# Flamingo block on one core: first sequence's queries moved tile to tile, keys split first, one query stack moved, transfers reordered

## The reference

```python
qs = relu(layernorm(x)).reshape(bs, ts, 16, 32)
ks = vs = relu(ctx).reshape(bs, ts, 16, 32)
att = softmax(einsum('bthf,byhf->bhty', qs, ks) / sqrt(32))
out = einsum('bhty,byhf->bhtf', att, vs).reshape(bs, ts, -1)
x = x + tanh(g_xattn) * relu(out @ ffn_w.T + ffn_b)
# feed-forward part, on n = layernorm(x) and n one token earlier
xr, xk = mu_r * n + (1 - mu_r) * n_prev, mu_k * n + (1 - mu_k) * n_prev
x = x + tanh(g_ffn) * sigmoid(xr @ W_r.T) * (square(relu(xk @ W_k.T)) @ W_v.T)
```

## Time and profile before

| what | us |
|---|---|
| median of 3 runs | 2684.31 |
| profiled execution, its own time | 2686.47 |
| its span | 2684.7 |
| TensorE matmul busy | 2597.9 (97%) |
| VectorE busy | 2282.9 (85%) |
| ScalarE busy | 1695.4 (63%) |
| GpSimd busy | 1162.9 (43%) |

### The profile page before, as it was taken

One profiled execution on the slowest core, in us unless ns is written; L12 is line 12 of the kernel. 1 busy time (PEld: TensorE's weight loads), 2 busy tenths in 40 slices (PEclk: granted clock), 3 DMA queues, 4 the chain that ended last, 5 costly groups with the idle time before them and its releaser, 6 DMA issues. The chain is left out here.

```text
span 2684.7 us, 66755 instructions
## 1 busy us (share of the span) xinstructions
PE 2597.9 (97%) x20354; PEld 2074.9 (77%) x20354; DVE 2282.9 (85%) x4109; ACT 1695.4 (63%) x3531; POOL 1162.9 (43%) x902
## 2 busy tenths in 40 slices
PE   3799999999999999999999999999999999999998
PEld 2577778787787787787787778778778778787776
DVE  6688888888888889888888888888888888888875
ACT  4466666666666666666666666666666666666663
POOL 0144444444444444444444444444444444444434
PEclk9799999999999999999999999999999999999999
DMA  9787777777777778778778778787787787777751
GB/s 256 210 215 228 215 213 230 222 212 229 221 209 233 223 208 234 218 209 234 223 209 234 218 211 232 211 222 224 214 227 222 211 231 222 211 228 220 209 153 44
DMA packets 523216, 576.78 MB, mean 215 GB/s; under 512 B 191264, under 2 KB 422688, under 8 KB 523168
## 3 DMA queue, kind: packets, MB, share of 16 engines
q1 hardware_dynamic: 369648, 340.71, 46.5%
q10 hardware_dynamic: 153520, 235.46, 30.1%
HBM read 373.56 MB, written 201.33 MB: 214 GB/s over the span
## 5 line engine op out<-in xcount | busy, mean ns | idle before, releaser
L618 ACT ACTIVATE probs<-bank 128x512 f32<-128x512 f32 x1024 | 610.2, 596 | 523.2 <-PE bank L1103 519.7
L858 DVE TENSOR_REDUCE m_nat<-bank 128x2 fp32r<-128x512 f32 x1024 | 689.2, 681 | 76.5 <-PE bank L1091 76.3
L1091 PE MATMUL bank<-k_st,q_st 96*128 96x256 f32 x2048 | 435.1, 295 | 37.5 <-ACT bank L630 26.2
L877 DVE RECIPROCAL o_val<-bank 128x256 f32<-128x256 f32 x192 | 336.7, 1754 | 138.8 <-PE bank L1129 138.8
L1091 PEld LDWEIGHTS bank<-k_st,q_st 96*128 96x128 f32 x2048 | 362.8, 193 | 108.0 <-ACT bank L630 40.1
L1103 PE MATMUL bank<-q_st,k_st 97*128 97x256 f32 x2048 | 426.2, 290 | 8.6 <-DMA q_st<-m_t 8.2
L1103 PEld LDWEIGHTS bank<-q_st,k_st 97*128 97x128 f32 x2048 | 357.3, 191 | 85.5 <-issue 23.3
L464 POOL TENSOR_TENSOR xm<-xm 128x512 f32<-128x512 f32 x128 | 157.1, 1227 | 463.0 <-ACT xm L677 462.0
L630 ACT ACTIVATE bank<-bank,m_nat 128x256 f32<-128x256 f32 x512 | 227.6, 444 | 136.5 <-DVE m_nat L858 136.2
L431 POOL TENSOR_TENSOR o_lo<-o_mv,o_hi 128x512 fp32r<-128x512 f32 x128 | 168.6, 1317 | 304.5 <-ACT o_hi L640 302.1
L1146 PE MATMUL bank<-xk_hi,w_hi 128*128 128x256 f32 x1024 | 294.9, 288 | 1.0 <-DVE th L940 1.0
(11 more groups left out here) (94 smaller groups left out, 5945.8 us busy)
## 6 DMA issues: line engine op xcount, KB each, us to landing
q_st<-q_dram ACTq DMA_DIRECT2D x256, 256.0 KB, 4.8
k_st<-k_dram SPq DMA_DIRECT2D x256, 256.0 KB, 4.7
k_raw<-ctx_t_dram SPq DMA_DIRECT2D x256, 128.0 KB, 5.1
q_st<-q_dram ACTq DMA_DIRECT2D x256, 128.0 KB, 2.9
k_st<-k_dram SPq DMA_DIRECT2D x256, 128.0 KB, 5.0
o_dram<-o_val SPq DMA_DIRECT2D x256, 128.0 KB, 2.1
o_mv<-o_dram SPq DMA_DIRECT2D x1024, 32.0 KB, 3.1
x<-x_dram ACTq DMA_DIRECT2D x64, 512.0 KB, 6.7
```

The costliest lines, as they stand in the source:

```text
L618: nc.scalar.activation(probs[:, n // GR % 2, n % GR, :, :].rearrange("p v t -> p (v t)"), st_bank[n % 2][:, :], ACT.Exp).then_inc(exp_read ...
L858: nc.vector.tensor_reduce(m_nat[:, c % 2, n % GR, :], s_bank[n % 2][:, :].rearrange("p (u y) -> p u y", u=NU), AX_X, ALU.max, negate=True) ...
L877: nc.vector.reciprocal(o_val[:, c % 2, :], pv_bank[:, T:2 * T]).then_inc(rden_ready, 1)
L1091: mm = nc.tensor.matmul(s_bank[n % 2][:, T * u:T * u + T], q_st[0:QK, c, g, P * u:P * u + P], k_st[0:QK, c, g, :], start=True, stop=True)
```

## The change

The change has five parts.

1. The stack of query group 0 of sequence 0 is no longer written to DRAM and read back. Twelve DMAs on ScalarE's queue take rows from `q_high` (eight) and `q_raw` (four) straight to `q_st`, one for each head and each of the three places. The halving of group 0 is done by itself first (`q_hi_first`, `q_lo_first`), on both ScalarE and VectorE. `q_copy(1, ...)` waits until these DMAs have read.
2. `stack_q(i, 3)` goes, in every iteration, from behind `exponent(i, 0)` to behind `sum_exp(i, 7)`.
3. `k_halve(0)` becomes the first thing of ScalarE's iteration -2 and `k_low(0)` follows `norm_1(0)`; `k_halve(1)` and `k_low(1)` go from iteration -1 into iteration 0 (behind `sum_exp(0, 6)` and `head_max(0, 9)`).
4. SyncE's opening is reordered: the first keys are written before `load_x(1)`, and `stack_k(0, 0)` is issued before the other groups are written; `stack_k(0, 2)` and `move_m(0, 0)` come before `load_k(1)`.
5. In iteration 0, `stack_k(1, 1)` directly follows `stack_k(1, 0)`, `load_x(3)` follows `write_o(0, 0)`, and the two `read_o` of the first tile go ahead of `move_m(1, 0)`, the first of them ahead of `write_o(0, 1)`.

```diff
@@ SyncE @@
+            def write_k_first(b, par):
+                sp.wait_ge(k_hi_ready, b + 1)
+                sp.wait_ge(k_lo_ready, b + 1)
+                for half, tile in enumerate((k_high, k_raw)):
+                    sp.dma_start(k_dram[par, 0, half].rearrange("f g t -> (f g) t"),
+                                 tile[:, 0, :]).then_inc(k_first, 16)
...
+                    if first_sequence(b) and c == 1:
+                        sp.wait_ge(k_written, 32)
                     sp.dma_start(k_st[0:2 * HD, c, :, :].bitcast(F32),
...
-                    if first_sequence(b) and c == 0:
-                        sp.wait_ge(k_written, 32)
@@ opening @@
                     load_k(0)
                     load_w(range(0, 4))
+                    write_k_first(0, par)
                     load_x(1)
+                    stack_k(0, 0, par)
                     write_k(0, par)
                 elif i == -1:
-                    stack_k(0, 0, 1 - par)
                     stack_k(0, 1, 1 - par)
+                    stack_k(0, 2, 1 - par)
+                    move_m(0, 0)
                     load_k(1)
-                    move_m(0, 0)
-                    stack_k(0, 2, 1 - par)
                     load_x(2)
...
                     stack_k(1, 0, 1 - par)
+                    stack_k(1, 1, 1 - par)
                     load_k(2)
                     move_m(0, 3)
                     load_w(range(6, 7))
                     write_o(0, 0)
-                    stack_k(1, 1, 1 - par)
                     load_x(3)
+                    read_o(0, 0, 0)
                     write_o(0, 1)
                     stack_k(1, 2, 1 - par)
+                    read_o(0, 0, 1)
                     move_m(1, 0)
                     load_w(range(7, 8))
-                    read_o(0, 0, 0)
-                    read_o(0, 0, 1)
@@ ScalarE @@
+                        act.wait_ge(q_hi_first, 1)
+                        for row in (0, HD):
+                            for g in range(GR):
+                                act.dma_start(q_st[row:row + HD, 0, g, :].bitcast(F32),
+                                              q_high[g:P:GR, 0, :]).then_inc(q_stacked[0], 16)
+                        act.wait_ge(q_lo_first, 1)
+                        for g in range(GR):
+                            act.dma_start(q_st[2 * HD:QK, 0, g, :].bitcast(F32),
+                                          q_raw[g:P:GR, 0, :]).then_inc(q_stacked[0], 16)
...
             def iteration(i, par):
+                if isinstance(i, int) and i == -2:
+                    k_halve(i + 2)
                 exponent(i, 0)
-                stack_q(i, 3, par)
                 sum_exp(i, 6)
+                if isinstance(i, int) and i == 0:
+                    k_halve(i + 1)
                 exponent(i, 1)
                 split_high(i, 6, 1)
                 sum_exp(i, 7)
+                stack_q(i, 3, par)
...
-                k_halve(i + 2)
+                if not (isinstance(i, int) and i < 0):
+                    k_halve(i + 2)
@@ VectorE @@
                 head_max(i, 9)
+                if isinstance(i, int) and i == 0:
+                    k_low(i + 1)
                 stats_1(i + 2)
...
                 norm_1(i + 2)
+                if isinstance(i, int) and i == -2:
+                    k_low(i + 2)
...
-                k_low(i + 2)
+                if not (isinstance(i, int) and i < 0):
+                    k_low(i + 2)
@@ TensorE @@
-                        pe.wait_ge(q_stacked[c], 32 * (b + 1))
+                        pe.wait_ge(q_stacked[c], 32 * (b + 1) + (16 * (3 * GR - 2) if c == 0 else 0))
```

More of the change, by code:

```diff
@@ L145, in flamingo_block @@
         q_copied = sem("q_copied")
-        q_first = sem("q_first")
+        q_hi_first = sem("q_hi_first")
+        q_lo_first = sem("q_lo_first")
         q_written = sem("q_written")
@@ L266, in write_k @@
                     sp.wait_ge(k_lo_ready, b + 1)
[L267 to L273, removed]
+                    groups = slice(1 if first_sequence(b) else 0, CH)
                     for half, tile in enumerate((k_high, k_raw)):
@@ L559, in write_q @@
                 if on(b):
-                    act.wait_ge(q_hi_ready, b + 1)
-                    act.wait_ge(q_lo_ready, b + 1)
                     groups = slice(0, CH)
@@ L565, in write_q @@
                         groups = slice(1, CH)
-                        for half, tile in enumerate((q_high, q_raw)):
-                            act.dma_start(q_dram[par, 0, half].rearrange("f g t -> (f g) t"),
-                                          tile[:, 0, :]).then_inc(q_first, 16)
+                        act.wait_ge(q_hi_first, 1)
[7 more added lines that the diff above has]
+                                          q_raw[g:P:GR, 0, :]).then_inc(q_stacked[0], 16)
+                    act.wait_ge(q_hi_ready, b + 1)
+                    act.wait_ge(q_lo_ready, b + 1)
                     for half, tile in enumerate((q_high, q_raw)):
@@ L573, in stack_q @@
             def stack_q(b, c, par):
-                if on(b):
-                    if first_sequence(b) and c == 0:
-                        act.wait_ge(q_first, 32)
-                    else:
-                        act.wait_ge(q_written, 32 * (b + 1))
+                if on(b) and not (first_sequence(b) and c == 0):
+                    act.wait_ge(q_written, 32 * (b + 1))
                     act.dma_start(q_st[0:HD, c, :, :].bitcast(F32), q_dram[par, c, 0]).then_inc(q_stacked[c], 16)
@@ L593, in q_copy @@
                     after(act, q_written, 32 * b)
+                    if isinstance(b, int) and b == 1:
+                        act.wait_ge(q_stacked[0], 16 * 3 * GR)
                     nc.scalar.activation(q_raw[:, :, P * u:P * u + P],
@@ L600, in q_halve @@
                     act.wait_ge(q_copied, NU * (b + 1))
-                    nc.scalar.activation(q_high[:, :, :].bitcast(F32R), q_raw[:, :, :], ACT.Copy).then_inc(q_hi_ready, 1)
+                    groups = slice(0, CH)
+                    if first_sequence(b):
+                        groups = slice(1, CH)
+                        nc.scalar.activation(q_high[:, 0, :].bitcast(F32R), q_raw[:, 0, :],
+                                             ACT.Copy).then_inc(q_hi_first, 1)
+                    nc.scalar.activation(q_high[:, groups, :].bitcast(F32R), q_raw[:, groups, :],
+                                         ACT.Copy).then_inc(q_hi_ready, 1)
             def k_halve(b):
@@ L839, in q_low @@
                 if on(b):
+                    groups = slice(0, CH)
+                    if first_sequence(b):
+                        groups = slice(1, CH)
+                        dve.wait_ge(q_hi_first, 1)
+                        nc.vector.tensor_tensor(q_raw[:, 0, :].bitcast(F32R), q_raw[:, 0, :], q_high[:, 0, :],
+                                                ALU.subtract).then_inc(q_lo_first, 1)
                     dve.wait_ge(q_hi_ready, b + 1)
-                    nc.vector.tensor_tensor(q_raw[:, :, :].bitcast(F32R), q_raw[:, :, :], q_high[:, :, :],
-                                            ALU.subtract).then_inc(q_lo_ready, 1)
+                    nc.vector.tensor_tensor(q_raw[:, groups, :].bitcast(F32R), q_raw[:, groups, :],
+                                            q_high[:, groups, :], ALU.subtract).then_inc(q_lo_ready, 1)
             def k_low(b):
```

## The result

The changed kernel took 2700.47 us, median of 4 runs (2699.91 to 2701.48), beside 2686.38 for the kernel before in the same measurement (2683.58 to 2691.25): ratio 1.005 with an interval of 1.0028 to 1.0072. That is 14 us slower, where 4 us faster was predicted. The profiled executions show 13.4 us of it (spans of 2698.1 and 2684.7). A name like `q_st<-q_dram` reads: tile `q_st` is written from `q_dram`.

The account below looks back on a forecast made before the run. It took TensorE, matmuls filling 97% of the span, as the bound behind a start of about 130 us. Successive opening shifts ended at 4 us, the moved stack adding nothing: 2684.31 median to 2680.3 us, range 2670 to 2687.

Parts of the forecast that it names:

- The moved stack, every iteration (part 2): Stack of query group 3 issued later each iteration: lands in time, costs nothing, at most 0.1 us either way.
- rival C: Moved stack's second DMA takes over 6.2 us, first score of group 3 waits in 61 iterations: 2698 us, chance 0.07.
- The twelve query DMAs: ScalarE's queue at the start: 0.45 us an issue, 5.2 to 8.3 us in all, hidden behind TensorE's transposes.
- First scores at 25.7: Start of sequence 0: first scores released by the transposes instead of the keys, about 2.4 us sooner than 28.06.
- Score 4: Sequence 0: its key stack no longer queues behind group 0's, start at 29.7 instead of 31.46, 1.7 us gained.
- Score 6: Sequence 0: work on sequence 1's keys leaves the path, start at 34.3 instead of 37.06, 2.7 us gained.
- the late keys: Iteration 0: sequence 1's keys hold ScalarE and VectorE; head 10's maximum at 46.2 instead of 47.64, 1.4 us left.
- Keys of group 1, sequence 1: Iteration 1: earlier key stack removes TensorE's 4.57 us wait; VectorE comes next, gain 3.3 us.
- Reads ahead of the maxima: Iteration 1: TensorE's maxima wait ends between 75.2 and 77.6; score 7 comes 4.8 to 2.4 us sooner, 4 taken.
- Rival A, the clock: Shorter stalls keep the matmul clock up between 62 and 127 us, 7.9 us more gained: 2672.4 us, chance 0.12.
- Rival B: Opening queues, by twelve issues, late `load_x(1)` or `move_m(1, 0)`, take the gain back: 0 to 1 us, 2684, chance 0.17.
- the -4 us of the sum: Whole kernel: the opening's shift of 4 us runs through to the full TensorE and comes off the median.

Follow-up runs that it names:

- e2: The kernel before with part 2 alone, the stack of group 3 moved behind `sum_exp(i, 7)`: 2696.26 us, ratio 1.0055.
- e3: The kernel before with `stack_q(i, 3)` moved only halfway, behind `sum_exp(i, 6)`: 2682.72 us, ratio 1.0004.
- e9: The kernel before with `stack_q(i, 3)` moved later still, behind `exponent(i, 2)`: 2774.88 us, ratio 1.0338.
- e11: The kernel before with `stack_q(i + 1, 0)` moved from behind `exponent(i, 3)` to behind `exponent(i, 5)`, from iteration 1 on: 2733.71 us, ratio 1.0175.
- e5: The changed kernel without parts 1 and 2, first queries through DRAM again: ratio 1.0 [0.9989, 1.0011] against the kernel before.
- e1: The changed kernel without part 2, `stack_q(i, 3)` back behind `exponent(i, 0)`: 2685.43 us, ratio 1.001 against the kernel before.
- e7: The kernel before with `stack_k(1, 1)` early and `move_m(1, 0)` kept ahead of both reads in SyncE's opening: 2683.01 us, ratio 0.9994.
- e6: The kernel before with part 5 alone: ratio 0.9999 [0.9988, 1.001].
- e16: The kernel before with part 1 alone, the twelve direct query DMAs: ratio 0.9999 [0.9987, 1.0012].
- e13: e11 with one more wait, GpSimd's `o_low(i - 1, 1)` waiting for `norm_1(i + 2)`: 2680.2 us, ratio 0.9975 against the kernel before.
- e4: e2 with `read_o(i - 1, 1, 1)` issued ahead of the store of the output: 2829.97 us, ratio 1.0565 against the kernel before.

## Why the prediction was wrong

**The step that failed: "The moved stack, every iteration (part 2) ... nothing".** I asked two things of the moved stack: does it land in time (it does: 8.4 against 12.45 us, so rival C did not happen, though its 14 us look like it), and does it hold ScalarE. I did not ask who shares the DMA engines in its new place. Those are the 128 KB write and the 4 x 32 KB read behind it, a chain with 0.6 us of slack. A DMA share of 0.35 over 3 us was read as room; it was the gap ahead of that chain. The place was off as well. I let the second DMA leave 0.4 us behind the end of the sums, which is 0.5 us behind the issue of the write (1021.47); but the issue does not wait for the sums to end. In the iteration shown it left at 1025.57, the sums ended at 1026.45, and so it stood 0.6 us ahead of the write (1026.15). e2 (+14 us alone), e3 (nothing when it lands earlier), e9 (+92 us when it hits the read) and e11 (read 2.0 us sooner when other bytes go away) show it from both sides; of e9's loss some part is the clock and the late stack, as told there.

**The twelve query DMAs: cost too low, and the upper bound too.** Taken as 0.45 us each, with 5.2 to 8.3 us in all; they took 5.12 + 3.48 = 8.6 us, 0.64 each for the eight and 0.87 for the four, gaps between them included. `move_m` was the nearer row, not the read from DRAM. The rule weighed there (the Trainium skill, DMA: Bandwidth & Descriptors, Rules for kernel authors) pointed this way, and the trace agrees: twelve small transfers cost more than the two pairs they replace, 8.6 us of the queue against 0.34 + 0.67 + 0.34 + 1.09 = 2.4 us, though by their issue time.

**First scores at 25.7:** 28.05, against 28.06. The keys were early as predicted, but the direct queries came in their place: ScalarE's copies and splits behind the twelve issues were late (e5: 24.6 without them). **Score 4** gained nothing (31.48 for 31.46; 29.7 predicted): its wait is now for the stack of the queries, behind the twelve issues. **Score 6** came 1.0 us sooner, of the 2.7; that is inside the scatter (e1, with the same opening, has 37.05). That the late keys hold ScalarE was right in kind and larger than thought: `k_raw` waited 3.2 us until 42.07, and head 10's maximum came at 48.82, 1.2 us later than before instead of 1.4 sooner.

**Keys of group 1, sequence 1:** right, that wait is gone. **Reads ahead of the maxima:** right that the wait stays, wrong in size. The wait ended at 79.50, 1.9 us above my upper end and 3.1 later than before: the write landed 5.0 us after its issue at 70.77, and that issue was itself behind four reads until 70.72, where I had 68. So score 7 came at 81.15 instead of 77, and the 4.57 us that went came back in the next wait, 7.17 us where the earlier trace rows have 2.55. e7, without it, gains 4.1.

**Rival A, the clock:** did not happen. From 89.5 and from 110 us the granted clock is still 0.57 and 0.54, and from 60 to 140 us 40.8 us are at 1.2 GHz as before; less than 15 would have been its sign. **Rival B** names the right mechanism for the opening; it gave 0 to 1 us of gain, and the shift at sequence 2 is 1.1 us of loss, which one execution cannot tell from none. The opening without part 1 (e5: 1.0 [0.9989, 1.0011]) is no gain, and the -4 us of the sum is not there; e1 puts the loss of parts 1, 3, 4 and 5 at 0.3 to 5 us.

**Sum by what was measured:** part 2, 14 us (e2); the rest, 3 us (e1). Together 17 against 14 measured, which fits within the intervals (2 to 6 us either way). In the profile part 2 is 0.16 us in each of 60 iterations, 10 us; against five kernels that leave the middle alone (e1, e5, e6, e7, e16: 40.42 to 40.48 us) it is 10 to 14.

Open: in e9 the read lands 2.0 us later and in e2 0.8, with the same 384 KB; I did not take apart how much of it is the place against the loads of x1 and v. Nor is it shown why TensorE waits for a row of maxima in a few iterations behind the moved stack, some 0.06 of the 0.16 us. And the differences of 1 to 3 us of the opening parts are read from one execution each, and the timed intervals hold them no better than ±0.1%.

## What to carry to other kernels

When a DMA is moved, its own deadline is the easy half: find the next transfers on the engines that someone waits for, and their slack, from issue to landing to the last instruction that needs them; a low mean share just ahead of such a chain is not free room. When a step is put ahead of a small row that the bottleneck waits for, add up every landing in front of it, not the issue lengths alone. And when an input comes sooner, see what its consumer then runs beside: e11 lost 50 us with its read 2 us sooner, and one wait that keeps two engines apart took the loss away. Last, take the scatter of a few unchanged kernels before reading a shift of 1 us off one trace.

## What the runs showed of the hardware that was not expected

- `norm_1` on VectorE, 128x512 float32 from on-chip memory to on-chip memory, takes 0.73 us at the least, and beside GpSimd's tensor_tensor up to 2.75 us. In e11 the 7 of the 128 that no GpSimd instruction overlaps take 0.79 us at most, and in e13, where 86 are free of one, 0.82; every one above 1.0 us is overlapped. The instructions of its line in e11 (least, median and most, in ns):

```profile
L836 DVE TENSOR_SCALAR q_nat<-x_ln,mv,rstd x128: 725/1285/2746, 8.7 to 2545.4; 128x512 f32<-128x512 f32 x128
```

With the wait of e13 the same row is:

```profile
L838 DVE TENSOR_SCALAR q_nat<-x_ln,mv,rstd x128: 722/782/1586, 8.8 to 2524.7; 128x512 f32<-128x512 f32 x128
```

The Trainium skill (SBUF — State Buffer, Who interferes with whom) says that VectorE and GpSimd share one pair of ports under an exclusive lock, that tensor_scalar can enter a mode that takes it, and that the other engine then waits for the whole instruction. The trace agrees: in the iteration shown under e11 the slow pair starts while `o_lo` runs and ends at 1771.77, just behind GpSimd's next instruction (1768.87 + 2.41 = 1771.28).
- A DMA that takes 32 rows from one on-chip tile to another occupied the issuing queue 0.64 or 0.87 us on the mean, gaps included (one issue 0.60 to 1.31), one of 32 KB from DRAM 0.43 us.
- Between 180 and 2600 us some waits of TensorE for `o_lo`, of 1.6 to 2.6 us, were followed by a granted clock of 1.2 GHz (e4, 71.7 us in all; e9, 17.1 us). The kernels before and after have no such stretch there.
- 384 KB in flight took a 128 KB write from 1.7 to 3.1 us (e2), and moved the landing of a 4 x 32 KB read by 2.0 us either way (e9, e11).
